# Feed-forward gate and up in three column chunks (512, 512, 384), with a PSUM bank each and one broadcast transfer per scale set

## What is computed

```
x = x + xattn(layernorm(x), ctx, ctx, ...)         # 16 heads of 32, 77 context rows, causal mask
x = x + ffn(layernorm(x), w_gate, w_up, w_down)    # 512 -> 1408 -> 512

def ffn(x, w_gate, w_up, w_down):
    gate = fp4_linear(x, w_gate)
    y    = fp4_linear(x, w_up)
    h    = silu(gate) * y
    return fp4_linear(h, w_down)

def fp4_quant_dequant(x):        # both operands of fp4_linear, in blocks of 16 along the last dim
    scale = max(max|x| / 6, 1e-12) ; xn = x / scale
    idx = searchsorted(_MID, |xn|)
    return _GRID[idx] * sign(xn) * scale
```

## Time and profile before

| | us |
|---|---|
| median of 3 runs | 1173.37 |
| lowest and highest | 1172.9, 1174.16 |
| the profiled execution | 1174.72 |
| its span on the core | 1172.9 |
| mean granted TensorE clock | 0.996 of full speed |

### The profile page before, as it was taken

How to read it: one execution, slowest core, us unless ns; L and a number is a source line. 1 busy time by engine, 2 the same in 40 slices (tenths; PEclk the granted TensorE clock), 3 DMA queues, 4 the chain that set the end, 5 groups by cost and what they waited for, 6 DMA issues and landing times.

```text
span 1172.9 us, 21792 instructions
## 1 busy us (share of the span) xinstructions
PE 1152.6 (98%) x6916; PEld 1044.1 (89%) x6916; DVE 970.2 (83%) x1609; ACT 479.4 (41%) x1201; POOL 179.6 (15%) x305
## 2 busy tenths in 40 slices
PE   7899999999999999999999999999999999999998
PEld 6688888888888889999999999999999999999997
DVE  6778888888888887898888888888888888888865
ACT  3556656566665642333332333333233223333321
POOL 2433333333333310100000000000000000000000
PEclk8999999999999999999999999999999999999999
DMA  7133233333434326563445445444534544453442
GB/s 240 35 101 104 86 102 99 100 105 99 143 123 160 120 88 216 128 109 78 91 97 93 84 83 101 83 90 90 101 72 93 99 88 88 84 105 74 83 85 45
DMA packets 139473, 119.26 MB, mean 102 GB/s; under 512 B 91637, under 2 KB 102981, under 8 KB 139180
## 3 DMA queue, kind: packets, MB, share of 16 engines
q1 hardware_dynamic: 139436, 118.83, 42.9%
HBM read 74.47 MB, written 24.94 MB: 85 GB/s over the span
## 4 chain that ended last, share of the span: by engine, by line
PE 82%; DVE 6%; ACT 6%; issue 3%; POOL 1%; DMA 1%; DVEq 0%; SPq 0%; POOLq 0%; ACTq 0%
PE g_ps L176 7%; PE g_ps L177 7%; PE u_ps L176 7%; PE g_ps L178 7%; PE u_ps L177 7%; PE u_ps L178 7%; PE d_ps L1442 6%; PE d_ps L1443 6%; PE d_ps L1441 6%; PE o_ps L791 4%; ACT probs L904 3%; PE s_ps L729 2%; PE w_ps L176 2%; PE s_ps L768 2%; PE q_ps L177 2%
## 5 line engine op out<-in xcount | busy, mean ns | idle before, releaser
L176 PE MATMUL g_ps<-wguh,xnh 128*128 128x352 f32 x496 | 162.8, 328 | 0.0
L176 PE MATMUL u_ps<-wguh,xnh 128*128 128x352 f32 x496 | 159.9, 322 | 0.5 <-DVE hid L1582 0.5
L177 PE MATMUL g_ps<-wgul,xnh 128*128 128x352 f32 x496 | 160.2, 323 | 0.0
L178 PE MATMUL g_ps<-wguh,xnl 128*128 128x352 f32 x496 | 159.8, 322 | 0.0
L177 PE MATMUL u_ps<-wgul,xnh 128*128 128x352 f32 x496 | 159.8, 322 | 0.0
L178 PE MATMUL u_ps<-wguh,xnl 128*128 128x352 f32 x496 | 159.6, 322 | 0.0
L904 ACT ACTIVATE probs<-s_ps,nsmax 128x77 f32<-128x77 f32 x512 | 113.7, 375 | 93.1 <-DVE nsmax L996 93.1
L1582 DVE TENSOR_TENSOR hid<-u_ps,silu 128x352 f32<-128x352 f32 x128 | 67.0, 523 | 77.8 <-PE u_ps L178 75.5
L1443 PE MATMUL d_ps<-wd,hql 128*128 128x512 f32 x330 | 129.0, 391 | 0.0
L1442 PE MATMUL d_ps<-wd,hqh 128*128 128x512 f32 x330 | 128.9, 391 | 0.0
L1441 PE MATMUL d_ps<-wd,hqh 128*128 128x512 f32 x330 | 128.4, 389 | 0.0
(11 more groups left out here) (177 smaller groups left out, 2524.0 us busy)
## 6 DMA issues: line engine op xcount, KB each, us to landing
scale_wide<-st_dram SPq DMA_DIRECT2D x248, 88.0 KB, 3.4
xin<-in_x_dram SPq DMA_DIRECT2D x32, 256.0 KB, 2.8
x_dram<-x SPq DMA_DIRECT2D x32, 256.0 KB, 2.2
xin<-x_dram SPq DMA_DIRECT2D x32, 256.0 KB, 2.7
out_dram<-y SPq DMA_DIRECT2D x32, 256.0 KB, 2.1
scale_wide<-st_dram SPq DMA_DIRECT2D x248, 32.0 KB, 1.8
w_wide<-ws_dram SPq DMA_DIRECT2D x30, 256.0 KB
wd_dram<-wd_out SPq DMA_DIRECT2D x11, 512.0 KB, 3.6
```

Source lines behind the costliest of these rows:

```text
L176: pe.matmul(out, lh, rh, start=(i == 0), stop=False)
L177: pe.matmul(out, lh, rl, start=False, stop=False)
L178: last = pe.matmul(out, ll, rh, start=False, stop=(i == n - 1))
```

## The change

Gate and up go in three column chunks of 512, 512 and 384 instead of four of 352. Each chunk has a bank of its own for gate and one for up (six banks; the four of `hq_ps`' two halves and the old pairs are used up for it), so a chunk's bank is reused by the same chunk of the next tile. The scale transpose goes into `xn_ps`, and the transposes of the last tile into `g_ps`. ACT writes silu straight into the columns of `hid`, and DVE multiplies in place; ACT therefore waits until hid of the tile before has been divided (`z_ready`). The sixteen broadcast transfers of a tile become two. The lists are reordered, and the two parts of the last tile are 1024 and 384 columns wide.

```diff
-GU_N = 352
-GU = FF // GU_N
+GU_COLS = [(0, 512), (512, 1024), (1024, FF)]
+GU = len(GU_COLS)
...
-        silu = sb("silu", [P, 2, GU_N])
...
-        g_ps = ps("g_ps", [P, 2, 512])
-        u_ps = ps("u_ps", [P, 2, 512])
-        hq_ps = ps("hq_ps", [P, 2, 4, P])
+        g_ps = ps("g_ps", [P, GU, 512])
+        u_ps = ps("u_ps", [P, GU, 512])
...
-        FIRST_PART, LAST_PART = Part(None, 2 * GU_N), Part(2 * GU_N, None)
+        FIRST_PART, LAST_PART = Part(None, GU_COLS[1][1]), Part(GU_COLS[1][1], None)
...
+        def gate_of(c):
+            lo, hi = GU_COLS[c]
+            return g_ps[:, c, 0:hi - lo], slice(lo, hi)
...
-                for b in range(P // BLK):
-                    sp.dma_start(scale_wide[b * BLK:(b + 1) * BLK, FC:SC, :].rearrange("p c k -> p (c k)"),
-                                 st_dram[b:b + 1, FC * P:SC * P].to_broadcast([BLK, EC * P])).then_inc(x_wide_loaded, 16)
+                sp.dma_start(scale_wide[:, FC:SC, :].rearrange("p c k -> p (c k)"),
+                             st_dram[:, FC * P:SC * P].unsqueeze(1).to_broadcast([P // BLK, BLK, EC * P])).then_inc(x_wide_loaded, 16)
...
-                if reached(GU * t + c - 1):
-                    pe.wait_ge(silu_ready, GU * t + c - 1)
-                split_matmuls(pe, g_ps[:, c % 2, 0:GU_N], [
+                total, cols = gate_of(c)
+                if reached(t):
+                    pe.wait_ge(silu_ready, GU * (t - 1) + c + 1)
+                split_matmuls(pe, total, [
...
             def iteration(a):
+                early = isinstance(a, int) and a < 3
                 if valid(a) and reached(a):
                     gate(a, 0)
+                if looped(a - 1) and not early:
+                    scales_transposed(a - 1)
+                if valid(a) and reached(a):
                     up(a, 0)
-                third = isinstance(a, int) and a == 2
-                if looped(a - 1) and not third:
+                if looped(a - 1) and early:
                     scales_transposed(a - 1)
...
-                if reached(GU * t + c - 1):
-                    act.wait_ge(hid_ready, GU * t + c - 1)
-                act.activation(silu[:, c % 2, :], g_ps[:, c % 2, 0:GU_N], ACT.Silu).then_inc(silu_ready, 1)
+                if reached(t):
+                    act.wait_ge(hquant.z_ready, t)
+                total, cols = gate_of(c)
+                act.activation(hid[:, cols], total, ACT.Silu).then_inc(silu_ready, 1)
...
-                dve.tensor_tensor(hid[:, c * GU_N:(c + 1) * GU_N], u_ps[:, c % 2, 0:GU_N], silu[:, c % 2, :],
-                                  ALU.mult).then_inc(hid_ready, 1)
+                lo, hi = GU_COLS[c]
+                dve.tensor_tensor(hid[:, lo:hi], up_of(c)[0], hid[:, lo:hi], ALU.mult).then_inc(hid_ready, 1)
...
                 if h:
                     hquant.block_max(dve, hid[:])
+                if direct(a) and not (isinstance(a, int) and a == 2):
+                    x_low(a)
...
-                if direct(a + 1) and not second:
-                    x_low(a + 1)
```

More of the change, by code:

```diff
@@ L1550, in iteration @@
                     hq_high(a - 2)
+                if x is not None and reached(a):
+                    f.centre(act, x)
                 if valid(a):
@@ L1644, in iteration @@
                 h, x = looped(a - 1), rounded(a)
-                second, third = (isinstance(a, int) and a == one for one in (1, 2))
+                first, second = (isinstance(a, int) and a == one for one in (0, 1))
                 done = a
@@ L1664, in iteration @@
                     hquant.add_magic(dve, done)
+                    grid(a - 1)
+                if x is not None and not first:
+                    f.norm_stats(dve, x)
                 if valid(a) and not second:
                     gate_times_up(a, 0)
-                if h:
-                    grid(a - 1)
-                if x is not None:
+                if first:
                     f.norm_stats(dve, x)
-                if valid(a):
                     gate_times_up(a, 1)
-                if not reached(a):
                     first_low()
-                if third:
+                if second:
+                    gate_times_up(a, 1)
+                if looped(a - 2):
                     hq_low(a - 2)
```

96 lines of the change are left out of this document (46 added, 50 removed).

## The result

The changed kernel takes 1179.26 us, median of 7 runs (1177.28 to 1181.25), against 1173.49 (1171.54 to 1174.49, 7 runs) for the kernel before beside it. The ratio is 1.0049, 95% interval 1.0038 to 1.0059. It is slower by 5.8 us; 4.8 us less had been forecast.

What follows compares the result with a forecast made beforehand. It took PE's stream of matmuls in the feed-forward as the bound: 32 tiles x 0.19 = 6.1 us saved, 1.3 lost at the start, so 1173.4 - 4.8 = 1168.6 us, with a range of 1164.3 to 1172.4.

Steps and rivals of the forecast that it cites:

- What bounds the kernel: Feed-forward: a stream of PE matmuls without waits in the loop; a tile costs 22.94 us by distances between starts.
- the chunks: Gate and up per tile: 512s at 228.4 ns, 384s at 172.5, so 15.23 us instead of 15.42, 0.19 less.
- a sign of being wrong: Profile after: a 512 in gate or up above 230 ns would show the forecast wrong.
- The first rival: Gate and up: excess belongs to their operands or banks; 512 costs 231 ns, no tile saving, 1174.7 us; chance 0.16.
- The rule cited beside it: Matmul gap: columns over 2.4 plus 2.5 ns; 24 fewer matmuls save 0.06 us a tile, leaving 1172.8 us.
- The start: Feed-forward's first tiles: waits of 2.6 us instead of 1.3, a loss of 1.3, between +0.5 and -3.
- The broadcasts: Merged scale transfers: half the DMA engines, about 3.2 us for x and 7 for hid, hidden.
- SP is on no chain in the loop: SP's queue in the loop: the 6 us saved by fewer issues are worth nothing by themselves.
- DVE and x_low: Loop: DVE's own loop 20.6 to 20.8 us, under PE's tile; x_low ends some 4.3 us before the next tile.
- the second rival: DVE's list in each tile: waits for late scales, slower, about 1195 us at one us; chance 0.07.
- The end: Last tile's stretch after the loop: no change, give or take 0.5 us.
- The range: Whole kernel: 1164.3 to 1172.4 us holds 8 in 10 of all cases.

Runs made afterwards that it cites:

- e6: Changed kernel with 384 bytes left free ahead of the x halves, so they start where gate and up weights do modulo 512; 1169.85 us, ratio 0.9975.
- e3: Changed kernel; in loop tiles gate chunks 0 and 1 and down's first four chunks read other operands, output not the reference's; 1177.99 us, one run.
- e5: Changed kernel; in loop tiles five groups of gate and up load other stationary operands, output not the reference's; 1176.45 us, one run.
- e2: Kernel before, four chunks of 352 kept, with only each scale set's broadcast merged into one transfer; 1173.12 us, ratio 1.0.
- e12: Changed kernel with x halves placed by 384 bytes, third down-weight load queued earlier, and 288 bytes ahead of the query weights; 1166.0 us, ratio 0.9933.
- e9: Changed kernel with x halves placed by 384 bytes, third down-weight load queued earlier, and 320 bytes ahead of wd; 1166.6 us, ratio 0.995.
- e1: Changed kernel with each scale set again spread by eight transfers of one block row each; 1175.67 us, ratio to before 1.0018.
- e10: Changed kernel; in loop tiles gate and up load stationaries from a gate-weight row at chosen distances, output not the reference's; 1176.29 us, one run.

## Why the prediction was wrong

**What bounds the kernel** was right: PE's stream of matmuls, no wait in the loop, a tile's time as the sum of its distances of starts. The step from narrow to wide failed at the price.

**The step that failed: the chunks.** "I take 228.4, between the two." The two were down (227.9) and the output product (229.2). Both pair a stationary with a streamed operand at distance 0. Gate and up pair the x halves with the gate weights at distance 128, and there a 512 costs 232.2, above the 230 that the text itself names as a sign of being wrong. The 384 was drawn between 352 and 512 and came out at 175.7 instead of 172.5. The term was 15.23 us and measured 15.47; 0.19 saved per tile became 0.05 lost. Over 32 tiles that is 7.7 of the 10.7 us between forecast and result. Of the other 3.0 the waits and the clock of the start have about 1.5 (2.8 in the profiled execution, 1.3 forecast); the rest is not explained. e6 shows the step from the other side: with the x halves placed at distance 0, the instructions as they were and the tensors behind the gap shifted together, the tile costs 22.74, the forecast's price to 0.01 us, and the time falls by 9.4.

A row that would have warned was in the trace of before: q_ps from wqh and xnh, the only 512-column product of the x halves, at 233 ns. I priced by shape and by neighbourhood in time. With 233 for the 512, the same sum saves nothing on a tile. It is not the same pair, though: the streamed operand is another, at distance 288 and not 128, and that both distances are dear is chance. The row shows that a 512 can cost 233 here; it could not show that gate and up would.

**The first rival** named this mechanism ("their operands, their banks"), with 231 and 173.5, a tile that saves nothing, and 1174.7. It had 0.16. I weighed it down with the 229.2 of the output product, since that stood among the same chunks; it has other operands, and does not speak against the rival. Banks have no part in it: e3 and e5 change the price in the same slots by operands alone. Even the rival was 1.2 ns too low for the 512 and 2.2 for the 384. The rule cited beside it, of the Trainium skill ("TensorE: Matmul & The Clock Gate", section "Back-to-back issue gap"), would give 215.8 ns for a 512; the page calls it the gap of an isolated matmul, and no row of this case comes near it.

**The start.** A loss of 1.3 us was forecast, between +0.5 and -3; that stretch was 3.0 longer in the profiled execution, 0.2 of it by its four dearer tiles and the rest from other causes. The transpose did not wait (1.0 forecast). Gate(2, 0) waited 0.65 (1.3 forecast) and gate(3, 0) for nothing of DVE (0.3 forecast). What cost was wd's third load, which the text names nowhere: 2.0 us of wait and 1.4 of lower clock. It was in reach. The broadcasts were rightly found to run on half of the DMA engines (share 0.51, 193 GB/s) and followed to the scales they carry. These took longer than forecast, 3.9 us instead of 3.2 for x and 12.0 instead of 7 for hid from issue to landing (4.5 and 9.9 in the loop tile above), and still nobody waited for them. They were not followed to what shares the queue. In the list of SP's program load_down(2) stands between the two broadcasts. No wait in the loop contradicts "SP is on no chain in the loop"; at the start SP is on one. The Trainium skill's rule on the outermost dimension ("DMA: Bandwidth & Descriptors", section "Rules for kernel authors") thus mattered in a place where I had not asked what else flies. e2 qualifies that: with the merged transfers alone the loads come later too, and nobody waits for them.

**DVE and x_low** were as forecast: no wait of PE in the loop, 0.70 us of DVE's idle time ahead of line 152 (0.8 forecast), x_low done 4.1 us ahead of the next tile (4.3 forecast). So the second rival (DVE waits for the scales) did not come. The result is slower, the side it had 0.08 for, but by another mechanism.

**The end** was given as 0 ± 0.5 and came at -0.4. Right.

**The arithmetic** has two slips, neither of weight: 15.10 and 0.15 are 15.25 and not 15.23, and today's waits of the start are 0.7 + 0.5 = 1.2 and not 1.3.

**The range**, 1164.3 to 1172.4, took a 512 from 227 to 229.2. The first rival's 231 was outside it, though the two had the same standing in the trace: no row showed the x halves with the gate weights at 512 columns. An unknown price between 227 and 231 or more, times 48 times 32, is 6 us or more. It belonged into the range.

## What to carry to other kernels

Price a matmul by a row with the same pair of operands, or one whose two operands start at the same distance, and not only by shape; where no such row exists, put the dearest row of that shape into the range. When a change makes one instruction wider, look where its two operands start: here 384 unused bytes were worth 9.4 us, more than the 6.1 that the forecast had for the chunk width. And ask whether anything else bounds the stage: in the attention the same remedy made the matmuls cheaper and not the time (e12). When a transfer gets slower but stays hidden, go through the queue it stands in and ask of every neighbour, in the first iterations too, who waits for it.

## What the runs showed of the hardware

- The distance between starts of 512-column matmuls (each with its own load of 128 x 128) depends on how far apart stationary and streamed operand start, modulo 512 bytes: 226.7 ns at distance 0, 231.5 to 233.0 at 128, 233.3 at 320 (after, e3, e5, e6). At the lower clock it does not show: there the starts are 427 ns apart at distance 128 (after, gate(3, 0)) and at distance 0 (e6, the same group). Moving the stationary by 128 bytes inside one tensor turned 227 into 233 and brought back single matmuls of 240.
- At distance 0, behind a group of another width or distance, three to ten matmuls are unsettled (224 to 236 ns) before the even 227 (before, e6, e9). Bringing all operands to one place moved this from gate to down (e9) and did not remove it.
- Behind a single 128 x 120 transpose the first start is 85 ns dearer, whatever the width: 318 ns instead of 232 for a 512 (after), 244 instead of 160 for a 352 (before), on average over 25 tiles.
- An idle PE of 1.9 to 2.7 us was followed by a stretch at the lower clock, 0.50, in after, e1, e5 and e6 (waits of 2.0, 1.9, 2.4 and 2.7 us). Waits of 2.2 and 1.7 us at the same place in e3 and e10 were followed by a clock of 1.00 throughout, and a gate(3, 0) of 2.79 us. So the fall is not certain at this length, and where it came it cost 1.4 to 1.7 us more.
- A 1 MB load issued between two broadcasts that run on half of the DMA engines landed one half early and the other half with the second broadcast: 12.7 us (after) and 12.0 (e2) instead of 5.7 (before).
- A DMA transpose queued behind the two broadcasts and the load of wd held SP for 8.29 us (after), 6.29 (e6) and 3.55 (e2); in the kernel before the same one took 1.41.
